# A window-attention block and a spectral mix on one core: the loop's products in runs of one tile shape, eight buffers in the last stage

## What is computed

```python
a = shifted_window_attention(x, ...)        # 4x4 windows, 4 heads of 16, cosine scores
x = x + layernorm(a, norm1_g, norm1_b)
h = gelu(x @ fc1_w.T + fc1_b) @ fc2_w.T + fc2_b
x = x + layernorm(h, norm2_g, norm2_b)
# second layer, along the rows of the image
trend = moving_average(x, 25)
xf = rfft(x - trend, axis=1)[:, :128]
ys = einsum('bmnc,cmk->bknc', xf, w_real + 1j * w_imag)
x = trend + irfft(pad(ys), n=256, axis=1)
```

## Time and profile before

| | |
|---|---|
| median of 3 runs | 8558.72 us (8556.22 to 12912.76) |
| the profiled execution | 8548.61 us, its span 8546.5 us |
| busy over the span | TensorE 94%, ScalarE 73%, VectorE 70%, GpSimd 63% |
| main loop | from 272 us (first transposes) to about 7296 us |
| last stage | from about 7303 us to the end |
| clock granted to TensorE | 0.971 of full over the span, 1.00 between 2000 and 7200 us |

### The profile page before, as it was taken

The page is one execution under the profiler, slowest core; times in us unless marked ns, Lnnn a source line. Parts: engine busy times, 40 slices in busy tenths (PEclk is TensorE's granted clock), DMA queues, the critical chain, the costliest instruction groups (busy, mean ns, idle before and its releaser), DMA issues.

```text
span 8546.5 us, 659317 instructions
## 1 busy us (share of the span) xinstructions
PE 8028.8 (94%) x293684; PEld 5312.2 (62%) x293684; DVE 5981.4 (70%) x8029; ACT 6209.3 (73%) x8530; POOL 5385.1 (63%) x5127
## 2 busy tenths in 40 slices
PE   8899999999999999999999999999999999787786
PEld 5556666666666666666666666666666665566565
DVE  1468888888888888888888888888888887222221
ACT  1478888888888888888888888888888888222221
POOL 0367777777777777777777777777777777000000
PEclk9799999999999999999999999999999999898898
DMA  3122222222222222222222222222222222799999
GB/s 99 53 50 58 58 58 59 59 59 59 59 58 59 59 59 59 58 59 58 59 59 59 58 57 57 58 59 59 59 58 59 59 58 55 269 317 329 330 318 334
DMA packets 1187111, 834.30 MB, mean 98 GB/s; under 512 B 633233, under 2 KB 1043217, under 8 KB 1182867
## 3 DMA queue, kind: packets, MB, share of 16 engines
q1 hardware_dynamic: 1182404, 698.61, 31.9%
q10 hardware_dynamic: 4608, 134.22, 3.7%
HBM read 412.97 MB, written 285.21 MB: 82 GB/s over the span
## 4 chain that ended last, share of the span: by engine, by line
PE 72%; SPq 14%; DMA 7%; issue 4%; ACT 2%; ACTq 0%; DVE 0%; POOL 0%; POOLq 0%; DVEq 0%
PE ps L501 12%; PE ps L479 11%; PE ps L581 10%; SPq L335 10%; PE ps L554 8%; PE ps L542 8%; PE ps L462 8%; PE ps L526 5%; PE ps L513 5%; DMA out<-arena 3%; DMA arena<-in_x 3%; PE ps L450 3%; SPq L346 2%; SPq L341 2%; PE ps L424 1%
## 5 line engine op out<-in xcount | busy, mean ns | idle before, releaser
L953 POOL TENSOR_TENSOR arena<-arena 128x512 f32<-128x512 f32 x1024 | 1043.5, 1040 | 894.2 <-PE ps L501 894.2
L479 PEld LDWEIGHTS ps<-arena 32*32 32x32 f32 x131072 | 1236.4, 106 | 508.4 <-issue 502.0
L501 PEld LDWEIGHTS ps<-arena 32*32 32x32 f32 x131072 | 1289.3, 103 | 292.8 <-issue 259.1
L501 PE MATMUL ps<-arena 32*32 32x16 f32 x131072 | 1424.4, 186 | 21.1 <-issue 19.5
L479 PE MATMUL ps<-arena 32*32 32x16 f32 x131072 | 1345.1, 180 | 23.3 <-issue 16.2
L805 DVE TENSOR_TENSOR arena<-ps,arena 128x768 f32<-128x768 f32 x1024 | 980.7, 958 | 370.1 <-PE ps L462 358.0
L581 PE MATMUL ps<-xch,amat 128*128 128x256 f32 x4096 | 924.3, 389 | 285.4 <-ACT arena L718 169.5
L462 PEld LDWEIGHTS ps<-arena 64*128 64x128 f32 x8192 | 649.1, 188 | 837.4 <-issue 825.5
L985 POOL TENSOR_TENSOR arena<-arena 128x512 f32<-128x512 f32 x512 | 713.5, 1394 | 696.2 <-DVE arena L844 696.2
L694 ACT ACTIVATE arena<-ps,arena 128x1024 f32<-128x1024 f32 x1024 | 1137.4, 1111 | 7.0 <-PE ps L542 0.4
L581 PEld LDWEIGHTS ps<-xch,amat 128*128 128x128 f32 x4096 | 786.6, 195 | 423.5 <-ACT arena L718 174.7
(11 more groups left out here) (89 smaller groups left out, 14288.3 us busy)
## 6 DMA issues: line engine op xcount, KB each, us to landing
arena<-in_x SPq DMA_DIRECT2D x4096, 32.0 KB
arena<-arena SPq DMA_DIRECT2D x1024, 128.0 KB
y<-ystripe SPq DMA_DIRECT2D x256, 512.0 KB
amat<-mix SPq DMA_DIRECT2D x512, 256.0 KB, 3.4
xch<-y SPq DMA_DIRECT2D x512, 256.0 KB, 4.0
out<-arena ACTq DMA_DIRECT2D x32, 4096.0 KB, 27.1
mix<-amat SPq DMA_DIRECT2D x64, 256.0 KB, 2.0
wri<-in_w_real SPq DMA_DIRECT2D x64, 64.0 KB, 1.8
```

The costliest lines, as they stand in the source:

```text
L479: ins = mm(S(sl)[r, c0 + e:c0 + 32:2], qT[r, sl, q, e:64:2], kT[r, sl, q, e:32:2], start=True, stop=True, tile_position=(32 * cg, 32 * cg))
L501: ins = mm(PV[32 * h:32 * h + 32, b, c0:c0 + N], vexp[r, sl, h, :, :], pT[r, sl, h // 2, h % 2, :], start=True, stop=True, tile_position=( ...
L953: tt(vexp.rearrange("p s h e d -> p (s h) e d")[:, :, e, :], qkv[ring(g, 4)][:, 2].rearrange("p s (h d) -> p (s h) d", h=HEADS), par[:, e: ...
```

## The change

The diff rewrites the order of the steps on every engine and what follows from it. On TensorE the two halves of `scores` stand together, and so do `project` and `second_layer`, both halves of `weighted`, and both halves of `project_qkv`; `turn_x` stands between `second_layer` and the first `weighted`. `VV` moves to banks 4 and 5. The two logarithms and the two inverse roots of the norms become one operation each over 1024 columns (`log_norms`, `root_norms`). `normed1` writes its result back into `D1`, and `add1` reads it there. The attention's steps on ScalarE, VectorE and GpSimd are done for other groups in a step. In the last stage `NB` goes from 4 to 8.

```diff
-        NB = 4
+        NB = 8
...
-        VV = MB
+        VV = ps[:, 4:6, :]
...
                 def turn_x(g):
                     if there(g):
                         need(pe, x_in, g, 16 * 8)
-                        after(pe, (gelu0, i6), (l1_sb, i5, i7), (xT_sb, before(g)))
+                        after(pe, (gelu1, i6), (qkvB_sb, before(g)))
...
+                def scores(g):
+                    if there(g):
+                        need(pe, qT_sb, g)
+                        need(pe, kT_sb, g)
+                        if there(i5) or there(i7):
+                            need_norms(pe, l12_sb, i5, i7)
+                        else:
                             after(pe, (oT_sb, i4), (biased, before(g)))
-                            settled(pe)
...
                 def project(g):
                     if there(g):
                         need(pe, oT_sb, g)
-                        need(pe, dn1_sb, before(g))
+                        need(pe, x1_sb, before(g))
...
-                        after(pe, (xT_sb, i0), (gelu0, i6), (l1_sb, before(g), before(h)))
+                        if there(i3):
+                            need(pe, oT_sb, i3)
...
-                scores(i2, 0)
+                scores(i2)
                 project(i4)
-                turn_x(i0)
-                scores(i2, 1)
                 second_layer(i6, 0, fc2a_ps)
                 second_layer(i6, 1, fc2b_ps)
+                turn_x(i0)
+                weighted(i3, 0, pvA_ps)
+                weighted(i3, 1, pvB_ps)
                 project_qkv(i0, 0, MA, qkvA_ps)
-                weighted(i3, 0, pvA_ps)
+                project_qkv(i0, 1, MB, qkvB_ps)
                 variances(i4, i6)
-                project_qkv(i0, 1, MA, qkvB_ps)
-                weighted(i3, 1, pvB_ps)
-                first_layer(i5, 0, MB, fc1a_ps)
-                first_layer(i5, 1, MA, fc1b_ps)
+                first_layer(i5, 0, MA, fc1a_ps)
+                first_layer(i5, 1, MB, fc1b_ps)
 
             over_groups(pe, step, 1)
 
...
+                def log_norms(g, h):
+                    if there(g) or there(h):
+                        need_norms(act, var_ps, g, h)
+                        k = slice(0 if there(g) else 1, 2 if there(h) else 1)
+                        f(l12[:, k, :], VV[:, k, :], ACT.Ln, bias=eps).then_inc(l12_sb, 1)
+
+                def root_norms(g, h):
+                    if there(g) or there(h):
+                        need_norms(act, l12_sb, g, h)
                         need(act, dn1_sb, before(g))
-                        f(r1, l1, ACT.Exp, scale=-0.5).then_inc(r1_sb, 1)
-
-                def square2(g):
...
                 def normed1(g):
                     if there(g):
-                        need(dve, r1_sb, g)
+                        need_norms(dve, r12_sb, i5, i7)
                         need(dve, x1_sb, before(g))
-                        stt(dn1, D1, be1, r1, ALU.add, ALU.mult).then_inc(dn1_sb, 1)
+                        stt(D1, D1, be1, r12[:, 0, :], ALU.add, ALU.mult).then_inc(dn1_sb, 1)
...
-                        stt(x1T, dn1, g1, xTo[ring(g, 4)], ALU.mult, ALU.add).then_inc(x1_sb, 1)
+                        stt(x1T, D1, g1, xTo[ring(g, 4)], ALU.mult, ALU.add).then_inc(x1_sb, 1)
...
+                gelu(i6, 0, MA, fc1a_ps, fc2a_ps, gelu0)
+                gelu(i6, 1, MB, fc1b_ps, fc2b_ps, gelu1)
                 square(i1)
                 square1(i4)
-                gelu(i6, 1, MA, fc1b_ps, fc2b_ps, gelu1)
+                act.preload_act_table_set(EXP_SET)
+                log_norm(i1)
+                root_norm(i1)
                 keep_x(i0)
+                square2(i6)
+                keep_o(i3)
+                exponent(i2)
+                log_norms(i4, i6)
+                root_norms(i4, i6)
+                act.preload_act_table_set(GELU_SET)
...
-                sum_prob(i3)
-                turn_k(i2)
-                qkv_out(i1, 1, MA, qkvB_ps, qkvB_sb)
-                turn_q(i2)
                 normed1(i5)
+                add1(i5)
                 normed2(i7)
-                invert(i3)
-                add1(i5)
-                sum_squares(i1)
                 bias(i2)
                 turn_prob(i3)
-                clamp(i1)
                 maximum(i2)
                 gain2(i7)
+                sum_squares(i1)
+                clamp(i1)
+                turn_k(i1)
                 qkv_out(i0, 0, MA, qkvA_ps, qkvA_sb)
+                qkv_out(i0, 1, MB, qkvB_ps, qkvB_sb)
+                turn_q(i1)
+                sum_prob(i2)
+                invert(i2)
...
-                divide(i2)
-                add_o1(i0)
-                add_o2(i4)
-                shift(i1)
-                scale_norm(i0)
-                norm_k(i0)
-                norm_q(i0)
-                expand_v(i1)
-                add2(i6)
+                divide(i3)
+                add_o2(i5)
+                add_o1(i1)
+                shift(i2)
+                add2(i7)
+                scale_norm(i1)
+                norm_k(i1)
+                norm_q(i1)
+                expand_v(i2)
```

89 lines of the change are left out of this document (30 added, 59 removed).

## The result

The changed kernel takes 8688.6 us (8682.9 to 8693.6, four runs) where the one before took 8558.4 in the runs beside it: ratio 1.0153, 95% interval 1.0136 to 1.0171. One of the four runs of the kernel before took 12912.8 us, and the ratio leaves it out. The forecast was 8268. The loss is inside the 2% band but outside the measurement's uncertainty, and it has the other sign.

What follows compares the result with a forecast made beforehand. TensorE's queue was taken to bound the loop, 13.48 us a group. From the profiled 8548.6 us, 261 for the loop and 30 for the last stage gave 8258, plus 10 for the median: 8268, range 8180 to 8410.

Steps and rivals of the forecast that it cites:

- part 1: TensorE's loop: four joined pairs save changes of shape, 0.61 us a group in sum (0 to 0.8).
- `weighted` (1.49 + 1.35 - 0.13): TensorE's two `weighted` halves joined: both old run times less one change of shape, 2.71 us.
- feeding the long runs: Rival, chance 0.10: long joined `scores` and `weighted` runs are held up, 2.85 us each; 8529 us, half of it 8350 to 8400.
- part 2: ScalarE, VectorE and GpSimd keep up with TensorE's 12.73 us a group, with slacks of 0.25 to 0.5 us.
- its own move of `add1`: VectorE's `add1` reading one operand in PSUM no longer contends with GpSimd: 1.62 us becomes 0.71.
- Part 3: Loop: the wait for x stays, and 0.10 us a group (0 to 0.3) is given back; net 261 us saved.
- layout of 12.73: TensorE's group laid out anew from the start of `scores` after the four joins: 12.73 us.
- Part 4: Last stage with `NB = 8`: 2 to 7 us saved per batch, seven times; 30 us taken.
- charge of 4.9 us: Last stage, per batch: 2.1 MB more to load for the four further channels may cost 4.9 us.
- would show it: Signs in the profile after: a group of 12.8 to 12.95 us, seven runs, `scores` near 2.3, `weighted` near 2.7.

Runs made afterwards that it cites:

- a_loads_late: `a_quarters_joined` with SyncE's loads of x issued only after the first half of `project_qkv`: 8650.2 us.
- a_quarters: Changed kernel with `weighted` halves apart, `add2` last on GpSimd, y stored behind `scores` in four quarters, one a group: 8218.5 us, ratio 0.9601.
- a_quarters_joined: `a_quarters` with the `weighted` halves side by side again behind `turn_x`: 8649.7 us, ratio 1.0103.
- a_store_shift: Changed kernel with SyncE's store of y issued one group later, behind `scores` and before the loads of x: 8650.6 us, ratio 1.0109.
- b_join_pv: Kernel before with only the `weighted` halves joined, ahead of the variances: 9383.5 us, ratio 1.097.
- a_both_apart: Changed kernel with `turn_x` between the `weighted` halves and `scores` in halves around `project`: 9892 us, ratio 1.163.
- bn_quarters: Kernel before with `NB = 8` and y stored in quarters behind `scores`, its order of products untouched: 9640.1 us, ratio 1.126.
- a_pad: Changed kernel with one dead dense product (128x128 weights, 256 columns) between the `weighted` halves: 8732.7 us, ratio 1.0213.
- a_spread: Changed kernel with the first `weighted` half moved between the halves of `second_layer`, the other behind `turn_x`: 8557.0 us, ratio 1.0002.
- a_turn_between: Changed kernel with `turn_x` between the two `weighted` halves: 8641.6 us, ratio 1.0113.
- a_spread_shift0: Changed kernel with `weighted` halves apart and the store of y behind `scores`, `add2` left where the change put it: 8530.2 us, ratio 0.9960.
- b_nb8: Kernel before with only the last stage's `NB` taken from 4 to 8, loop untouched: 8493.8 us, ratio 0.9931.
- a_add2_late: Changed kernel with GpSimd's `add2` moved behind `expand_v` at the end of its row: 8655.9 us, ratio 1.0129.

## Why the prediction was wrong

**The products' terms (part 1).** Three of four joins went nearly as computed: `project` with `second_layer` 2.76 (2.73), `project_qkv` 1.53 at the full clock (1.50), `scores` 2.30 where no transfer runs beside it (2.26), though 2.50 in the mean. The method, losses at a change of shape read off the loads, was sound. The step that failed is "`weighted` (1.49 + 1.35 - 0.13)": it treated the halves as work that can stand end to end. The second half waits for `pvA_ps`, the end of the first; both write the same banks. Before, variances and `project_qkv` stood between and hid that. The wait stands in the code (`need(pe, pvA_ps, g)`). From the start of the last load of the first half to the start of the second half's first load 0.34 us pass in most groups; the group by line lists 106.7 us of waiting. The run's 3.11 us come apart so, as an estimate from three kernels: `scores`, of as many products, takes 2.30 alone; without loads beside it the joined weighted run takes 2.77 (`a_loads_late`), so 0.47 go with the wait; and the loads beside it add 0.34. The forecast's 2.71 had about 0.4 for the loads in it without saying so, since its two halves were read with loads beside them (apart, and with at most the start of the loads beside them, they take 2.43 in `a_quarters`). What it lacked is the wait.

**The rival "feeding the long runs"** had the right place and the wrong cause. It blamed the number of products in a run. `a_loads_late` shows that what holds a run up is SyncE's transfers beside it, and the earlier trace rows had these: 8.13 us of loads in the group with a store. Their position against the new layout was never drawn. The rival's sum was also wrong: its group of 13.46 leaves out the 0.14 of waiting that the 13.48 of before has in it. It should stand at 13.60, 0.12 a group slower than before. That makes 8590 us instead of 8529, with the other sign.

**The clock** was in no term. The table of before gave 1.00 between 2000 and 7200 us, and the sum kept it. It costs 0.26 us a group (97 of 458 groups, 1.23 us each): about 130 us, as much as the whole loss of the loop's steady part. The runs show it falling behind joined weighted runs (after, `a_quarters_joined`, `a_store_shift`, `b_join_pv`) and where TensorE waits 0.8 us or more in each group (`a_both_apart`, `bn_quarters`). Parting the halves with dense work ends it in that place (`a_pad`, `a_spread`), and so does taking the loads of x away (`a_loads_late`, 7 of 461). The length of the single run is not the condition. A weighted run of 2.82 us lost the clock in 23 of 115 groups of `a_store_shift`. `scores` at 3.15 us never lost it in the changed kernel, nor at 3.05 in `a_loads_late`, but at 3.0 it did in 51 of 116 groups of `a_spread`. What the condition is stays open. The changed kernel's groups at the full clock take 13.47 us, as long as the 13.48 of before: the wait and the transfers ate up what the joins saved, and the clock and the first groups turned the sign.

The Trainium skill, "TensorE: Matmul & The Clock Gate", section "Part 4: PE-mode transpose", says that products in transpose mode don't count as activity for the clock as others do. `a_turn_between` against `a_pad` agrees: `turn_x` between the halves left 116 stretches, one dense product left 1 in that place.

**The others' rounds (part 2).** `add1` at 0.75 and `normed1` at 0.74 were right, `divide` at 1.22 too. The prediction asked which of two operations meet in its own move of `add1`, and not which other pair the new rows bring together: `clamp` now starts while `add2` runs. These two rows are VectorE's and GpSimd's in one group of the changed kernel:

```profile
4013.42 1.21 DVE L811 TENSOR_SCALAR arena<-arena 128x64 f32<-128x64 f32 x1
```

```profile
4013.30 1.28 POOL L1000 TENSOR_TENSOR ystripe<-arena 128x512 f32<-128x512 f32 x1
```

ScalarE's chain was taken without it. In the changed kernel the copy of x is still done 0.4 us ahead of TensorE in the median, since `weighted` ends late; where `weighted` ends earlier, the slack is gone (15.3 us of waiting in 1000 in `a_turn_between`, 17.9 in `a_spread_shift0`). The Trainium skill, "SBUF — State Buffer", section "Who interferes with whom", lists this form among those that can take the port pair shared with GpSimd; 1.15 us with `add2` beside it and 0.195 without agree. The same section was read for `add1` and not for `clamp`.

**Part 3, given back 0.10 us (0 to 0.3).** The losses came to 1.0 us a group over the layout of 12.73, where the forecast allowed 0.24 (0.14 for x and 0.10): `weighted` 0.40, the clock 0.26, `scores` 0.24, and 0.03 each in `project` with `second_layer`, `project_qkv` and `first_layer`. In the loop's steady part, from the 17th `turn_x` to the last, a group takes 13.74 instead of 13.49, which makes 125 us in 495 groups; 60 more come in its first 16 groups, which take 322 us instead of 262, and some 9 around the loop. The first 16 are written out without a loop, and there TensorE waits more for its own instructions. The row of `scores` between 380 and 480 us, after and then before:

```profile
L477 PE MATMUL ps<-arena 32*32 32x16 f32 x1280 | 14.4, 185 | 13.7 <-issue 13.7
```

```profile
L479 PE MATMUL ps<-arena 32*32 32x16 f32 x1382 | 16.0, 183 | 6.2 <-issue 6.0
```

That this is the cause of those 60 us wasn't tried; `a_quarters` keeps 43 of them.

**Part 4** was right in kind and low in size: 7.5 us a batch by `b_nb8`, where 2 to 7 were the bounds and 30 in all was taken. Four channels at its own 1.95 us make 7.8, so next to nothing of the charge of 4.9 us for the larger load at a batch's end was seen.

**What was right, and what only looks so**: the limit on TensorE was read correctly. The group of 12.8 to 12.95 us that "would show it" is there in `a_quarters`, 12.83, but by another sum, and that is luck. Against the kernel before, the joins of `project_qkv` and of `project` with half of `second_layer` gave 0.17 and 0.09 there, `scores` 0.02, and the largest part, 0.33, came from `weighted`, whose halves are not joined, and have at most the start of the loads of x beside them. What stood between the forecast and the changed kernel were a wait, the place of the transfers and the clock, with a port behind them that costs once TensorE is faster. Single remedies for them moved the time by 33 to 131 us, of which only the largest stands well clear of the 30 us of a kernel whose clock falls; together they gave 470.

**Open**: what makes the clock fall behind one joined run and not behind another of the same length, why `b_join_pv` loses it in 260 groups where the changed kernel loses it in 97, and by what path a transfer slows a 32x32 run. The trace puts these gaps down to "issue", the supply of instructions, and no run separates that from the memory's ports.

## What to carry to other kernels

Joining runs of small products saves what a change of shape costs, and takes away the cover that the work between them gave: for each pair look for a wait that the first part's end must release, and for the engines whose results the moved run released. Draw the DMA queue's issues over the new layout, since many small products side by side are slowed by transfers beside them, and the same transfers cost nothing beside wide ones (`first_layer` stays at 1.92 in `a_loads_late` with the loads beside it). Before trusting a clock of 1.00 in a sum, ask what the new order puts side by side; and when a change with a sound budget disappoints, look for several small losses that hide each other, since mending one here moved the time by under 2% and all of them by 5.4%.

## What the runs showed of the hardware

- The granted clock falls in the middle of a loop in which TensorE is 98% busy by the trace: 0.52 between 4082.70 and 4086.00 us, behind `turn_x` and 256 products of 32x32 tiles with 16 columns. With one dense product of 0.63 us in their midst 1 of 97 such falls is left.
- How long such a run takes doesn't tell whether the clock falls: in `a_store_shift` it fell in 23 of 115 weighted runs of 2.82 us and in 55 of 345 of 3.10 us, and in `a_loads_late` never in or right behind a `scores` run of 3.05 us.
- A joined run of 256 such products takes 2.3 us alone, and with four or five of SyncE's transfers issued in it 3.15 (`scores` of the changed kernel).
- A VectorE `tensor_scalar` of 128x64 takes 0.195 us alone and 1.15 when it starts during GpSimd's addition of 1.28 us (`a_add2_late` against the changed kernel).
- The Trainium skill, "SBUF — State Buffer", section "Who interferes with whom", says that DMA never contends with a compute engine. At the ports that may be so. In this kernel TensorE's small products lost 0.75 us in a `scores` run to the loads beside it (`a_loads_late` against `a_quarters_joined`), and the measurement decides.
- A wait of 0.8 us in each group can cost far more than 0.8 us: `bn_quarters` took 2.3 us more a group than the kernel before; its groups at the full clock took 13.88, those touched by the lower clock 16.25.
